# Reordering the road into a causal attention: norm squares before spectral transfers, stacks from one queue, a tabled work order

## What is computed

```
h = E[x] + pos
h = h + linear_attention(layernorm(h))                 # 8 heads of 8
y = layernorm(h); r = rmsnorm(y) * ln1
q, k = rope(r Wq), rope(r Wk); v = r Wv                # 4 q heads, 2 kv heads of 16
a = softmax(causal(q k^T / 4)) v; x1 = y + a Wo
h = h + x1 + top-2-of-8 experts(rmsnorm(x1))
h = h + gated long convolution by FFT(layernorm(h))    # transfer function A from a small network
h = h + layernorm(h) W4 + b4
```

## Time and profile before

| | us |
|---|---|
| median of 3 runs | 383.98 (380.18 to 384.93) |
| the profiled execution | 387.35 |
| its span, first to last instruction | 385.6 |
| TensorE busy | 333.8 (87%) |
| VectorE (DVE) busy | 237.0 (61%) |
| ScalarE (ACT) busy | 144.2 (37%) |
| GpSimd (POOL) busy | 105.1 (27%) |
| mean granted TensorE clock | 0.929 |

### The profile page before, as it was taken

One profiled execution on the slowest core, in us unless ns is written; L12 is line 12 of the kernel. 1 busy time (PEld: TensorE's weight loads), 2 busy tenths in 40 slices (PEclk: granted clock), 3 DMA queues, 4 the chain that ended last, 5 costly groups with the idle time before them and its releaser, 6 DMA issues.

```text
span 385.6 us, 4537 instructions
## 1 busy us (share of the span) xinstructions
PE 333.8 (87%) x1675; PEld 184.8 (48%) x1675; DVE 237.0 (61%) x394; ACT 144.2 (37%) x238; POOL 105.1 (27%) x137
## 2 busy tenths in 40 slices
PE   1357877959899989778999999999989999899995
PEld 0124655522334442444775455554645555467744
DVE  1498775879887750115578455565467667764385
ACT  2123437330575658332156345554352112012260
POOL 5795000235421222200000142121001788900000
PEclk9998998975899999856979999999999999999998
DMA  7949200076000000000000000000000000000001
GB/s 273 300 147 417 116 0 0 2 121 126 1 3 0 2 4 0 2 0 0 2 0 1 0 2 0 3 0 0 3 0 2 0 0 2 0 0 0 2 1 54
DMA packets 6167, 15.27 MB, mean 40 GB/s; under 512 B 1282, under 2 KB 3714, under 8 KB 5506
## 3 DMA queue, kind: packets, MB, share of 16 engines
q1 hardware_dynamic: 5410, 14.27, 11.8%
q0 software_dynamic: 512, 0.53, 0.6%
q10 hardware_dynamic: 224, 0.20, 0.4%
HBM read 12.05 MB, written 0.52 MB: 33 GB/s over the span
## 4 chain that ended last, share of the span: by engine, by line
PE 64%; DVE 19%; ACT 7%; POOL 5%; issue 3%; DMA 1%; ACTq 0%; SPq 0%; DVEq 0%
PE ps L301 62%; DVE share L1268 2%; POOL e_lo L418 1%; DVE st L1224 1%; DVE arena L1467 1%; DVE rw L1400 1%; DMA idt<-ident 1%; PE ps L498 1%; DVE st L1231 1%; DVE xc L1232 1%; DVE sq L1240 1%; ACT arena L1045 1%; ACT sq L973 1%; POOL arena L484 1%; ACT L979 1%
## 5 line engine op out<-in xcount | busy, mean ns | idle before, releaser
L301 PE MATMUL ps<-arena 96*128 96x512 bf16 (+6 forms) x192 | 48.6, 362 | 5.2 <-DMA arena<-arena 3.6
L1092 ACT ACTIVATE arena<-ps 128x1024 f32<-128x1024 f32 (+3 forms) x48 | 37.9, 812 | 36.9 <-PE ps L301 36.2
L1400 DVE TENSOR_REDUCE rw<-ps 128x1 f32<-128x512 f32 (+3 forms) x78 | 45.7, 643 | 7.8 <-PE ps L301 7.8
L301 PE MATMUL ps<-bfc_s 128*128 128x512 bf16 (+2 forms) x173 | 44.3, 371 | 1.1 <-DVE tmp L1365 1.1
L301 PE MATMUL ps<-xs,e_hi 128*128 128x512 f32 x96 | 41.0, 427 | 0.2 <-ACT arena L1118 0.2
L1467 DVE TENSOR_TENSOR arena<-ps,arena 128x512 f32<-128x512 f32 x48 | 33.0, 691 | 11.2 <-ACT arena L1118 10.8
L301 PE MATMUL ps<-xs,e_lo 128*128 128x512 f32 x96 | 38.9, 406 | 0.0
L1118 ACT ACTIVATE arena<-ps 128x512 f32<-128x512 f32 x48 | 28.7, 598 | 26.1 <-PE ps L301 22.4
L301 PEld LDWEIGHTS ps<-arena 96*128 96x128 bf16 (+1 forms) x192 | 16.5, 103 | 37.0 <-DVE rw L1400 18.6
L301 PE MATMUL ps<-share,tu_s 128*128 128x384 f32 x96 | 32.5, 488 | 0.0
L301 PE MATMUL ps<-w,xT 128*128 128x128 f32 (+3 forms) x160 | 27.1, 357 | 3.0 <-DVE xT L1430 1.6
(11 more groups left out here) (236 smaller groups left out, 501.1 us busy)
## 6 DMA issues: line engine op xcount, KB each, us to landing
w<-wpack SPq DMA_DIRECT2D x1, 2152.5 KB, 10.5
arena<-arena SPq DMA_DIRECT2D x22, 96.0 KB, 2.8
arena<-tm SPq DMA_DIRECT2D x2, 1024.0 KB, 5.9
arena<-epack SPq DMA_DIRECT2D x1, 1540.0 KB, 11.1
arena<-rope SPq DMA_DIRECT2D x1, 1024.0 KB, 13.3
tu_s<-tu SPq DMA_DIRECT2D x2, 512.0 KB, 12.1
tk_s<-tk SPq DMA_DIRECT2D x2, 512.0 KB, 13.6
rp<-rpack SPq DMA_DIRECT2D x1, 678.5 KB, 4.1
```

Of the source, the lines that this page charges most:

```text
L301: return nc.tensor.matmul(o, l, r, start=start, stop=stop, **kw)
L1092: nc.scalar.activation(pt[:, n % PT_SLOTS, :, lo:512], ps[:, bank:bank + 2, lo:512], ACT.Exp, scale=HD ** -0.5).then_inc(S("exp_done"), 1)
L1400: V.tensor_reduce(top_view(m, part)[:, at:at + len(heads), i], src, AXX, ALU.max, negate=True).then_inc(S("ring_read"), 1)
```

## The change

- `EARLY_AF` goes from 7 to 5: five transfers before T2, four behind the queries. ACT squares the first half ahead of the `gt` copies and the second right behind them; its roots stand behind copies 0 and 1. The load of the exponential's table moves from before T2's copy to behind the last piece copy.
- The rounding of the expert weights goes in three parts of up to 1027 columns: before and behind the DVE's copy of T2, and behind the last rotation. `last_piece(6)`, which gives `q_pieces` 2, moves from before the rows to behind the DVE's first two row items. POOL's subtraction waits for all three parts.
- SP issues all 24 stack DMAs, in seven groups; the first rows wait for three of them (two q, one k). The DMA of the first `mrow` goes to ACT's queue.
- Eight fillers instead of four before the rows, behind the wait for `va2`, and one filler behind each row item ahead of the first `cols` item.
- Row items of a unit of four heads go by pairs of heads (12 instead of 11 in units 0 and 5, 80 in all). `ORDER` takes from tables how many ring items stand beside a step, how far `pv` lags, where the `y` items stand, and after how many row items a `top` stands. In the tail, `pv` 22 and 23 stand between `yT` and the first `o`.

```diff
-EARLY_AF = 7
+EARLY_AF = 5
...
+E_PART = 1027
...
-    for i, group in ((0, 4), (1, 2), (2, 1), (3, 1)):
-        for a in range(0, len(heads), group):
-            items.append((i, heads[a:a + group], c * 512, (i + 1) * P, 1))
+    for a in range(0, len(heads), 2):
+        pair = heads[a:a + 2]
+        items += [(i, pair, c * 512, (i + 1) * P, 1) for i in range(2)]
+        items += [(i, (hh,), c * 512, (i + 1) * P, 1) for i in (2, 3) for hh in pair]
...
-TOP_LAG = 4
+TOP_AFTER = (4, 3, 4, 5, 8, 3)
...
-    RING += _items[:TOP_LAG] + ([("top", _m - 1, 0)] if _m else []) + _items[TOP_LAG:]
+    RING += _items[:TOP_AFTER[_m]] + ([("top", _m - 1, 0)] if _m else []) + _items[TOP_AFTER[_m]:]
...
+RING_BESIDE = (2, 2, 2, 2, 2, 3, 0, 3, 1, 3, 2, 2, 3, 1, 3, 1, 2, 2, 3, 1, 3, 3, 2, 1,
+               0, 2, 1, 3, 0, 3, 1, 1, 2, 0, 0, 2, 2, 1, 0, 0, 1, 1, 3, 3, 1, 0, 0, 12)
+PV_BEHIND = (2, 3, 5, 5, 5, 7, 6, 6, 5, 6, 7, 4, 5, 6, 6, 5, 5, 5, 5, 4, 5, 4, 4, 5)
+Y_BESIDE = {36: [("y", 0, 0)], 45: [("y", 0, 1), ("y", 1, 1)], 47: [("yT", 1, 0)]}
+
+STACKED = (48, 48, 64, 32, 64, 64, 64)
+STACKS_OF = {(0, 0): (0,), (0, 6): (1,), (1, 0): (2,), (2, 0): (3,), (3, 0): (5, 6), (5, 0): (4,)}
+SLOT_STACKS = {0: (0, 1, 4), 1: (2, 5), 3: (3, 6)}
...
-    if _s >= PV_LAG and _s % 2 == 0:
-        ORDER.append(("pv", (_s - PV_LAG) // 2, 0))
-    for _ in range(min(len(_todo), ring_per_step(_s))):
-        ORDER.append(_todo.pop(0))
-    ORDER += y_items(_s)
-ORDER += [("pv", len(COL_STEPS) // 2 - _p, 0) for _p in range(PV_LAG // 2, 0, -1)] + [("y", 1, 0), ("yT", 0, 0), ("o", 0, 0)]
+    while _pairs < len(PV_BEHIND) and 2 * _pairs + 1 + PV_BEHIND[_pairs] <= _s:
+        ORDER.append(("pv", _pairs, 0))
+        _pairs += 1
+    ORDER += _todo[:RING_BESIDE[_s]]
+    _todo = _todo[RING_BESIDE[_s]:]
+    ORDER += Y_BESIDE.get(_s, [])
+ORDER += [("pv", _p, 0) for _p in range(_pairs, len(PV_BEHIND))]
+ORDER += [("o", 1, 0), ("y", 1, 0), ("yT", 0, 0), ("o", 0, 0)]
...
             sp.wait_ge(S("q_pieces"), 1)
             sp.wait_ge(S("copies"), 1)
-            stack_q(0, 0, S("stacks0"))
+            stack_q(0, 0, 0, 0)
+            stack_q(0, 0, 1, 0)
             sp.wait_ge(S("k_pieces"), 1)
             sp.wait_ge(S("copies"), 2)
-            stack_k(0, 1, S("stacks1"))
+            stack_k(0, 0, 0, 0)
+            stack_q(0, 0, 2, 1)
+            stack_q(0, 0, 3, 1)
+            stack_k(0, 0, 1, 1)
+            stack_k(0, 1, 0, 2)
+            stack_k(0, 1, 1, 2)
+            for hh in range(NH):
+                stack_q(1, 0, hh, 4)
             sp.wait_ge(S("q_pieces"), 2)
             sp.wait_ge(S("copies"), 3)
-            stack_q(0, 1, S("stacks1"))
-            stack_k(1, 0, S("stacks2"))
-            stack_k(1, 1, S("stacks2"))
-            stack_q(1, 1, S("stacks2"))
-            stack_q(1, 0, S("stacks3"))
+            for hh in range(NH):
+                stack_q(0, 1, hh, 2 + hh // 2)
+            for c in range(2):
+                for g in range(NKV):
+                    stack_k(1, c, g, 5)
+            for hh in range(NH):
+                stack_q(1, 1, hh, 6)
             for m, (b, c, heads) in enumerate(TOP_UNITS):
+                if m == 0:
+                    continue
                 sp.wait_ge(S("ring_read"), RING_ORDER.index(("top", m, 0)) + 1)
...
-            pool.wait_ge(S("e_split"), 1)
+            pool.wait_ge(S("e_split"), 3)
             pool.wait_ge(S("k_pieces"), 1)
             pool.wait_ge(S("q_pieces"), 2)
...
-            keep_warm(4, 1)
+            pe.wait_ge(S("va2"), 1)
+            keep_warm(8, 7)
...
-                if n == 0 and m in (0, 1, 3, 5):
-                    group = (0, 1, 3, 5).index(m)
-                    pe.wait_ge(S("stacks%d" % group), (96, 96, 128, 64)[group])
+                for group in STACKS_OF.get((m, n), ()):
+                    pe.wait_ge(S("stacks%d" % group), STACKED[group])
...
-            for kind, x, y in ORDER:
+            for at, (kind, x, y) in enumerate(ORDER):
                 if kind == "rows":
                     score_rows(x, y)
+                    if at < COLS_FROM:
+                        keep_warm(1, 7)
...
+            def squares_of(i, a):
+
+                act.wait_ge(S("centred"), 2 * (i - (i > 2)) + a + 1)
+                nc.scalar.activation(sq[:, 4 * a:4 * a + 4], xc[:, 4 * a:4 * a + 4], ACT.Square).then_inc(S("squared"), 1)
+
+            squares_of(1, 0)
             for s in range(2):
                 act.wait_ge(S("gf"), s + 1)
                 nc.scalar.copy(gt[:, s], ps[:, 4 + s]).then_inc(S("gt_done"), 1)
             nc.scalar.copy(gt2[:, 1:P], ps[:, 4, 1:P]).then_inc(S("gt_done"), 1)
             act.wait_ge(S("gf"), 3)
             nc.scalar.copy(gt2[:, 0:1], ps[:, 6, 0:1]).then_inc(S("gt_done"), 1)
+            squares_of(1, 1)
...
             for n in range(EARLY_AF):
                 af_copy(n, (2, 6, 4)[n % 3])
-
-                if n == 2:
-                    squares(1, xc)
+                if n == 0:
                     act.wait_ge(S("mean_squares"), NORMS["var2"])
                     nc.scalar.activation(st[:, 3], st[:, 2], ACT.Sqrt).then_inc(S("roots"), 1)
-                if n == 4:
+                if n == 1:
                     act.wait_ge(S("mean_squares"), NORMS["msq2"])
                     nc.scalar.activation(st[:, 6], st[:, 5], ACT.Sqrt).then_inc(S("roots"), 1)
-            next_function(ACT.Exp)
             evac(2, S("T2"), 1, S("xT2_lo"), scale=W("ln1"))
...
-            act.wait_ge(S("k_pieces"), 1)
-            act.wait_ge(S("copies"), 2)
-            for g in range(NKV):
-                act.dma_start(kst[0:MROW, g, 0:512], pieces_k[16 * g:16 * g + 16].rearrange("p n t -> p (n t)")).then_inc(S("stacks0"), 16)
-            for n in range(EARLY_AF, EARLY_AF + 2):
+            def late_copy(n):
                 af_copy(n, (2, 4)[(n - EARLY_AF) % 2])
+
+            late_copy(EARLY_AF)
+            late_copy(EARLY_AF + 1)
             act.wait_ge(S("v2"), 1)
             act.wait_ge(S("constants"), CONSTANTS["va2_ones"])
             nc.scalar.copy(va2[:, :, :, :, 0:HD],
                            ps[:, 7].rearrange("p (j b k d) -> p j b k d", j=NT, b=B, k=NKV)).then_inc(S("va2"), 1)
-            late = list(range(EARLY_AF + 2, 2 * NK + 1))
-            for n in late[:3]:
-                af_copy(n, (2, 4)[(n - EARLY_AF) % 2])
+            late_copy(EARLY_AF + 2)
             piece(5, 3, pieces_q1, Q_SLOTS, 0, qr[:, 512:N])
-            for n in late[3:4]:
-                af_copy(n, (2, 4)[(n - EARLY_AF) % 2])
+            late_copy(EARLY_AF + 3)
             piece(6, 3, pieces_q1, Q_SLOTS, 1, tmp[:, 512:N])
-            for n in late[4:]:
-                af_copy(n, (2, 4)[(n - EARLY_AF) % 2])
+            next_function(ACT.Exp)
             act.wait_ge(S("af_done"), 1)
             nc.scalar.copy(afx[:, 0], af[:, 0, 0]).then_inc(S("af_done"), 1)
...
+            act.wait_ge(S("ring_read"), RING_ORDER.index(("top", 0, 0)) + 1)
+            act.dma_start(qst[MROW:KROWS, 0, 0:NH], mrow[0:12 * NH, 0]).then_inc(S("top_rows0"), 16)
             for n, (k, j) in enumerate(COL_STEPS):
                 act.wait_ge(S("cols"), n + 1)
-                if n == 0:
-                    for group, value in enumerate((96, 96, 128, 64)):
-                        act.wait_ge(S("stacks%d" % group), value)
+                for group in SLOT_STACKS.get(n, ()):
+                    act.wait_ge(S("stacks%d" % group), STACKED[group])
...
             scale_rows(sq, x1, 7, S("n2"))
+
+            def split_experts(part):
+
+                dve.wait_ge(ld_e, 32)
+                at = slice(part * E_PART, min(NSPLIT, (part + 1) * E_PART))
+                V.tensor_copy(e_hi[:, at], e_raw[:, at]).then_inc(S("e_split"), 1)
+
+            split_experts(0)
             evac(3, S("T2"), 2, S("xT2_hi"), scale=W("ln1"))
+            split_experts(1)
...
             turn(2, 0, qr[:, 512:N], tmp[:, 512:N], [rope_s[:, x, 512:N] for x in range(2)])
+            split_experts(2)
             rest_of(5, qr[:, 512:N], pieces_q1, Q_SLOTS, tmp[:, 512:N])
-            last_piece(6, pieces_q1, Q_SLOTS, tmp[:, 512:N], S("q_pieces"))
-
-            dve.wait_ge(ld_e, 32)
-            V.tensor_copy(e_hi[:], e_raw).then_inc(S("e_split"), 1)
...
             for n, (kind, x, y) in enumerate(RING_ORDER):
                 bank = RING_BANKS[n % 3]
+                if n == 2:
+                    last_piece(6, pieces_q1, Q_SLOTS, tmp[:, 512:N], S("q_pieces"))
                 dve.wait_ge(S("ring"), n + 1)
```

32 lines of the change are left out of this document (11 added, 21 removed).

## The result

| us | before | after |
|---|---|---|
| median of 4 runs each | 384.46 (380.18 to 385.28) | 367.61 (366.72 to 368.89) |
| the profiled execution | 387.35 | 368.48 |
| its span | 385.6 | 366.7 |
| mean granted TensorE clock | 0.929 | 0.977 |

The ratio is 0.958 (95% interval 0.950 to 0.965): 16.9 us less between the medians, 18.9 between the two profiled executions. The forecast was 371.8 (364.5 to 378.5), faster. In three batches of later runs the kernel before took 385.37, 383.99 and 385.91 us. There is one profile of before, at a mean clock of 0.929; its other executions went from 0.921 to 0.959.

What follows compares the result with a forecast made beforehand. It took TensorE as the bound mid-attention, the DVE in the first rows, with stalls at either end. Terms 6.5 + 3 + 2.5 + 0.3 = 12.3 off 387.35 gave 375.0, scaled to the median 371.8 us (364.5 to 378.5).

Steps and rivals of the forecast that it cites:

- The head start: From second norm to first column steps: earlier transposes, stacks and rows bring the pair of weighted sums 6.5 us sooner.
- alone leaves the start: First rows: the change can't do nothing, since the DVE's 1.7 us rounding pass alone leaves the start.
- rival d: Stack DMAs: SP's issues stay slow, 382 us at 1.43 us each, 389 at 2.0; chance 0.04.
- rival c: First rows: head start spent on POOL and DMA, with a clock fall in the row stretch, 377.8 us; chance 0.16.
- The order table: Attention column steps: moved work fills TensorE's idle time, notably in steps 33 to 47; net 3 us (0.5 to 4.5).
- rival a: Column steps: bursts of three row items with three ring banks starve TensorE, 379.1 us; chance 0.13.
- The 9.9 us against 9.9: Steps 16 to 23: DVE and TensorE each have 9.9 us of work, so some of the gain comes back.
- The tail: End of attention: filled copy waits give 3.2 us, a held clock 5.8 more, an earlier fall loses 1.8 to 2.4; taken 2.5.
- rival (b): End of attention: the clock holds through the tail, total gain 18.6 us, 365.5 us; chance 0.15.
- The fillers and the router: Behind the tail: the 34 fillers end 0.7 us after the DVE's work; a better clock gives 0.3 us.

Runs made afterwards that it cites:

- e4: Changed kernel without the 22 fillers beside the first rows and with four instead of eight ahead of them: 368.53 us, ratio 0.963 to before.
- e2: Changed kernel with only the last work items of the tail in the old sequence: 372.85 us, ratio 0.975 to before.
- e3: Changed kernel with the old second norm (seven early transfers, squares behind the third copy): 373.81 us, ratio 0.980 to before.
- v1: Changed kernel with POOL's subtraction waiting for the third rest instead of the last query piece: 369.71 us, ratio 0.966 to before.
- e1: Changed kernel with the old work order, row-item grouping and tail: 381.39 us, ratio 0.992 to before.
- e6: Changed kernel with the expert rounding in one stretch behind the last query piece, ahead of the first row item: 365.63 us, ratio 0.955 to before.
- e5: Changed kernel with the two k stack DMAs of the first block issued by ACT again: 371.23 us, ratio 0.969 to before.
- e9: Old kernel with only the last eight work items in the new sequence: 376.63 us, ratio 0.982 to before.
- e8: Old kernel with one filler matmul behind each of column steps 33 to 45, 13 in all: 386.41 us, ratio 1.010 to before.
- e7: Changed kernel with the first two blocks' output transposes back beside column steps 16 and 32: 369.10 us, ratio 0.961 to before.
- v2: Changed kernel with POOL's subtraction in three pieces, the first before the last query piece, two after it: 366.26 us, ratio 0.955 to before.

## Why the prediction was right, point by point

**The head start (forecast 6.5, measured 7.4).** Each time that the forecast named, beside the measured one less the 2.17 us of the start-up: transposes 61.05, 61.13; first rotation product 64.05, 63.80; SP's first issue 71.5, 71.28; first rows 76.0, 76.56; first maximum 76.5, 77.00; top transpose 86.35, 86.87; first column step 90.2, 90.57; the weighted sums 102.7, 101.84. The middle ones are half a us late for one reason: the third stack DMA took 3.80 us to land (the chain above), where I had taken 3.1 from a median of 2.8 and a maximum of 4.4. The last is 0.9 early: from the top transpose on, before took 16.8 us and after 15.0. I had put 0.4 there. Of the 1.8 the full clock is 1.3: at a low clock the order of after takes 16.3 (e4, e2, e3). That the head start passes through is shown by e3 at equal clock, and up to the end of the attention once more by v1, whose 2.7 us at the top transpose are still 2.8 at the start of the last output projection.

Of the 7.4 the norm's own part is 3.6 (e3). Six stacks instead of three at the first row are 1.3 to 1.6 (e1), and the clock behind the top transpose 1.3 (e4). The 1 us that the forecast took at the first query product for a full clock is there (the rotation product comes 4.8 sooner than before), but e3 has it with the old norm too, so the change isn't shown to be its cause. The rounding pass of 1.7 us that "alone leaves the start" is worth nothing: e6 puts it back and is no slower. The move of the table load and of the first `mrow` DMA was undone by no run on its own.

**SP's issues (rival d, 382 to 389).** The two groups of after's stack DMAs, issue time in ns min/median/max:

```profile
L329 SPq DMA_DIRECT2D arena<-arena x16: 572/597/690, 73.4 to 88.9; - x16
```

```profile
L335 SPq DMA_DIRECT2D arena<-arena x8: 571/600/1090, 74.9 to 86.3; - x8
```

None is near the 1.7 us from which rival (d) decides. e5 shows that a second queue lengthens SP's issues, as the forecast had read from the earlier trace rows against the rule of the Trainium skill, "DMA: Bandwidth & Descriptors", section "Rules for kernel authors". It also shows what the forecast had not seen: ACT isn't idle there, and its copies are late behind its own DMAs.

**POOL (rival c, 377.8).** Its wait for POOL is there, 2.19 us of TensorE at the top transpose, but the forecast had it in its own sum (top transpose at 86.35). The clock didn't fall, and e4 shows what a fall costs: 1.3 us up to the end of the attention, where that rival had 2.

**The order table (forecast 3, measured 2.9 up to the last column step).** Of it 1.7 is idle time of TensorE (2.0 of 50.2 us before, 0.3 of 47.3 after, from the 109.22 and the 104.01 markers on). The other 1.2 is luck: the forecast had said that only idle time can be won, but the same items keep TensorE busy for 48.2 us before and 46.9 after, both at a granted clock of 1.00, and no run tells why. Of the three-item bursts (rival a, 379.1) the profile shows next to nothing: TensorE waits 0.2 us for the DVE's maxima from 92 to 137 us, 0.8 before. The 9.9 us against 9.9 that I had set against the table in steps 16 to 23 did not come back as a loss.

**The tail (forecast 2.5, measured 8.4).** This is the step that failed, and it failed in its size. The forecast split it rightly: 3.2 for the waits (3.0 measured) and either +5.8 or a loss of 1.8 to 2.4 for the clock. It then took a fall, since "the output transposes at 157.25 were the last dense work before it". The measured part is +5.4, rival (b)'s. The row that I read as a cause, light matmuls ahead of the fall, doesn't suffice as one: after has 32 such transposes together, at 146.16, in 3.68 us, all at full clock (the stretch 148 to 154 above has 1.00). What differs in e9, which changes nothing but the sequence, is that the three waits right behind the last column step are filled or shorter (0.39 us for 0.94). The forecast priced the waits and the clock as two things; in before, e1 and e9 they go together. They aren't one thing either: with all the waits in place e2 and e8 lose 1.6 and 1.8 us to the clock and not 5.4. What it takes ahead of the waits for the long fall is open.

**The fillers and the router (forecast 0.3, measured 2.2).** The 34 fillers ended 0.9 us sooner against the work ahead of them and the router's small products came out 1.2 sooner, both at a better clock. I had allowed 0.5 for it in rival (b) only. As this stage takes 15.9 us in e5, e7 and v2 with the new tail, the 2.2 are how this execution's clock fell, not a gain of the change that can be counted on.

**The total.** Sum 12.3, measured 18.9 in the profiled executions, though their start-ups differed by 2.2 the other way. That the median lies at 367.6 and inside the range is owed to the range having been drawn down towards rival (b); that rival had been given 0.15.

## What to carry to other kernels

Where TensorE's last stage alternates work and short waits for copies, price the waits twice: once as idle time, and once as the work behind them at half clock if the trace of before shows it there. Here 3 us of waits went with 5.4 us of clock in before, and with 1.6 and 1.8 in two kernels with other work ahead of them, so give the second price a range. A filler that keeps the clock up is worth only what TensorE's own pace is worth in that stretch and the next: here nothing up to the top transpose, which other engines set, and 1.3 us behind it. And before an instruction is moved onto an "idle" queue or started early, look at what stands behind it on that engine and which instruction of its neighbour reads the same memory.

## What was not expected of the hardware

- The DVE's subtraction of 512 columns with both inputs in SBUF took 3.94 us beside POOL's subtraction and 0.68 without; POOL's subtraction beside it wasn't slowed (5.60, 5.58), but its next one was (1.74, 1.27).
- SP's DMA issues took 0.60 us alone and 1.01 in the median (1.37 at most) while ACT issued two; the landing went from 2.9 us to 4.4.
- The same start-up code takes from 55.3 to 58.7 us, by the clock granted from 36 to 42 us (1.00 in e2, 0.68 in after, 0.50 in e7); two executions of after itself are 1.7 us apart (57.45, 55.71) before the changed code is reached. A gain of 1 to 2 us, as v2's and e6's, is read only at equal mean clock.
